# Cross attention on one core: every second exponential's bias on GpSimd, and the placing of the next queries split in two

## The reference

```python
q = (x @ Wq + bq).reshape(1, B * N, H, hd)
kv = (cond @ Wkv + bkv).reshape(1, -1, 2, H, hd)
q = _fq_sym(q * scale, axis=-1)          # rounded to 255 levels per row
k = _fq_sym(k, axis=-1)
v = _fq_sym(v, axis=2)
attn = jax.nn.softmax(jnp.einsum('bhqd,bhkd->bhqk', q, k), axis=-1)
attn = _fq_unsigned(attn, axis=-1)       # round(x / s) * s, s = row max / 255
out = jnp.einsum('bhqk,bhkd->bhqd', attn, v)
out = out.reshape(B, N, C) @ Wp + bp
```

## Time and profile before

| What | Value |
|---|---|
| Median of three runs | 994.36 us |
| The profiled execution's own time | 992.61 us |
| Its span in the trace | 990.7 us |
| Mean granted TensorE clock, share of full speed | 0.882 |
| VectorE busy, share of the span | 733.7 us, 74% |
| GpSimd busy | 564.7 us, 57% |
| ScalarE busy | 557.1 us, 56% |
| TensorE matmuls busy | 779.9 us, 79% |
| Stage of the 128 units (first score to last exponential) | about 653 to 849 us |
| VectorE, ScalarE, GpSimd busy from 740 to 760 us | 19.44, 16.98, 14.91 us of 20 |
| Granted clock from 740 to 760 us | 0.76 |

### The profile page before, as it was taken

The page is one execution under the profiler, slowest core; times in us unless marked ns, Lnnn a source line. Parts: engine busy times, 40 slices in busy tenths (PEclk is TensorE's granted clock), DMA queues, the critical chain, the costliest instruction groups (busy, mean ns, idle before and its releaser), DMA issues. The chain is left out here.

```text
span 990.7 us, 14021 instructions
## 1 busy us (share of the span) xinstructions
PE 779.9 (79%) x4673; PEld 500.3 (50%) x4673; DVE 733.7 (74%) x1291; ACT 557.1 (56%) x1028; POOL 564.7 (57%) x440
## 2 busy tenths in 40 slices
PE   4999999946877787778878978767777777789991
PEld 2554754425665666656763366623333333356551
DVE  4866258289999999999942555579999999454564
ACT  2324013278778777687741255479888888224540
POOL 3115200299999998999931033248777776315652
PEclk9999999969889989978989989967777777789996
DMA  5002030000000000000006000769999999422224
GB/s 175 1 6 81 1 133 2 0 1 1 1 0 1 1 1 1 1 0 1 1 1 229 0 1 1 266 120 176 186 182 167 172 174 173 83 86 75 78 74 159
DMA packets 149525, 69.61 MB, mean 70 GB/s; under 512 B 139003, under 2 KB 144909, under 8 KB 148302
## 3 DMA queue, kind: packets, MB, share of 16 engines
q1 hardware_dynamic: 147150, 62.42, 28.7%
q0 software_dynamic: 2304, 6.29, 2.1%
HBM read 27.46 MB, written 7.68 MB: 35 GB/s over the span
## 5 line engine op out<-in xcount | busy, mean ns | idle before, releaser
L749 POOL TENSOR_TENSOR r_pairs<-r_side_exp 128x945 f32<-128x945 f32 x128 | 225.2, 1794 | 0.0
L847 ACT ACTIVATE r_w<-r_w,r_scale 128x1001 f32<-128x1001 f32 (+1 forms) x128 | 144.9, 1135 | 71.8 <-DVE r_w L932 57.2
L1669 ACT ACTIVATE c_probs<-c_scores,c_bias,c_q_scale 128x1024 int16<-128x1024 f32 x128 | 154.2, 1205 | 30.0 <-DVE c_bias L1682 21.1
L804 PE MATMUL r_head_sum<-ident,r_w 128*128 128x128 f32 (+1 forms) x1024 | 136.7, 294 | 43.1 <-ACT ctxT L858 21.8
L1606 POOL CAST kv_parts<-c_probs 128x1024 bf16<-128x1024 int16 x128 | 132.4, 1041 | 54.7 <-ACT c_probs L1669 53.6
L1680 DVE TENSOR_REDUCE c_neg_max<-c_scores 128x1 f32<-128x1024 f32 x128 | 155.5, 1215 | 6.5 <-PE c_scores L1619 6.3
L804 PEld LDWEIGHTS r_head_sum<-ident,r_w 128*128 128x128 f32 (+1 forms) x1024 | 127.0, 155 | 61.0 <-issue 34.1
L1619 PE MATMUL c_scores<-c_kT,c_placed 128*128 128x512 bf16 x256 | 107.0, 513 | 49.5 <-ACT c_probs L1669 46.2
L924 DVE SCALAR_TENSOR_TENSOR r_chosen<-r_pairs,r_kept,r_z 128x1024 f32<-128x1024 f32 (+1 forms) x104 | 128.0, 1272 | 4.4 <-ACT r_pairs L837 2.5
L932 DVE TENSOR_TENSOR r_w<-r_pairs,r_chosen 128x1024 f32<-128x1024 f32 (+1 forms) x104 | 121.3, 1204 | 0.0
L780 PE MATMUL r_head_sum<-r_up,ctxT 128*128 128x256 f32 (+1 forms) x256 | 69.6, 439 | 22.5 <-ACT ctxT L858 22.5
(11 more groups left out here) (325 smaller groups left out, 1482.0 us busy)
## 6 DMA issues: line engine op xcount, KB each, us to landing
en_w<-in_w SPq DMA_DIRECT2D x1, 2992.0 KB, 12.1
ew_w<-in_w SPq DMA_DIRECT2D x1, 2992.0 KB, 12.3
ew_w_near<-in_w_near SPq DMA_DIRECT2D x1, 2176.0 KB, 21.3
r_up<-in_up SPq DMA_DIRECT2D x1, 2048.0 KB, 9.9
c_pT<-kv_parts SPq DMA_TRANSPOSE x128, 3.3
token_rows<-e_xn SPq DMA_DIRECT2D x2, 1024.0 KB, 5.8
e_row<-pick_rows SPq DMA_DIRECT2D x8, 256.0 KB, 4.2
zero_rows<-b_zeros SPq DMA_DIRECT2D x1, 1360.0 KB, 15.3
```

Of the source, the lines that this page charges most:

```text
L749: nc.gpsimd.tensor_tensor(pairs[:, v % MADE, BY_ACT * KEYS:].rearrange("p (a b) -> p a b", b=KEYS), a.broadcast_to([P, ROWS - BY_ACT, KEYS ...
L804: last = nc.tensor.matmul(head_sum[0:m, b // 4, (b % 4) * P:(b % 4 + 1) * P], w[:, v % RING, b * P:b * P + m], ident[:, :], start=(h == 0 ...
L847: nc.scalar.activation(w[:, v % RING, 0:COLS[f]], w[:, v % RING, 0:COLS[f]], ACT.Silu, scale=scale[:, t % 2, h:h + 1]).then_inc(silu_done, 1)
L1669: nc.scalar.activation(probs[:, u % RING, :], scores[:, u % SCORED, :, :].rearrange("p a b -> p (a b)"), ACT.Exp, bias=bias[:, t, h:h + 1] ...
```

## The change

Three things change.

1. In `attend` VectorE makes the bias of even units only. For odd units it makes the row maximum and signals `max_ready`; GpSimd makes the bias (`shift`), signals `pool_bias_ready`, and ScalarE waits for that. The bias of unit u+2 stands on GpSimd's stream behind the cast of unit u, for odd u; the one of unit 1 stands first.
2. The two copies of `place_queries` are parted: one before the cast of h = 4, one before that of h = 6. Each waits for the casts and the biases made so far.
3. Two semaphores go. VectorE's work on the decay waits for `phi_parts`, the first projection's relu, which stands behind the decay's exponential on ScalarE's stream. The keys' loads count on the same semaphore as the earlier weights, so that ScalarE and VectorE wait for the keys too.

```diff
-            dve.wait_ge(decay_exp, 1)
+            dve.wait_ge(phi_parts, 1)
...
-                sp.dma_start(keys[j * RETR:(j + 1) * RETR, :, j, :], i["keys"][j]).then_inc(keys_loaded, 16)
+                sp.dma_start(keys[j * RETR:(j + 1) * RETR, :, j, :], i["keys"][j]).then_inc(loaded, 16)
...
-            act.wait_ge(loaded, PRIVATE_LOADS)
+            act.wait_ge(loaded, PRIVATE_LOADS + 32)
...
-        PLACE_AT = 4
+        PLACE_AT = (4, 6)
...
+            def shift(u):
+                t, h = divmod(u, HEADS_C)
+                pool.wait_ge(max_ready, u // 2 + 1)
+                nc.gpsimd.tensor_scalar(bias[:, t, h:h + 1], neg_max[:, t, h:h + 1], s.q_scale[:, t, h:h + 1], LOG_LEVELS,
+                                        ALU.mult, ALU.add).then_inc(pool_bias_ready, 1)
+
+            shift(1)
             for u in range(UNITS_C):
                 t, h = divmod(u, HEADS_C)
-                if h == PLACE_AT and t + 1 < NT:
-                    pool.wait_ge(rounded_ready, u)
+                if h in PLACE_AT and t + 1 < NT:
                     if t >= 1:
                         pool.wait_ge(scored, HEADS_C * t)
-                    place_queries(nc, s, t + 1)
-                    pool.wait_ge(q_placed, 2 * (t + 2))
+                    own = PLACE_AT.index(h)
+                    pool.wait_ge(rounded_ready, u)
+                    pool.wait_ge(pool_bias_ready, (u + 2) // 2)
+                    place_queries(nc, s, t + 1, own)
+                    pool.wait_ge(q_placed, 2 * (t + 1) + own + 1)
                 pool.wait_ge(exp_done, u + 1)
...
                 nc.gpsimd.tensor_copy(rounded[:, u % ROUNDED, :], probs[:, u % RING, :]).then_inc(rounded_ready, 1)
+                if u % 2 == 1 and u + 2 < UNITS_C:
+                    shift(u + 2)
...
-                act.wait_ge(bias_ready, u + 1)
+                if u % 2 == 0:
+                    act.wait_ge(bias_ready, u // 2 + 1)
+                else:
+                    act.wait_ge(pool_bias_ready, u // 2 + 1)
...
-                chain.step(nc.vector.tensor_reduce(neg_max[:, t, h:h + 1], scores[:, u % SCORED, :, :].rearrange("p a b -> p (a b)"),
-                                                   AX.X, ALU.max, negate=True))
+                last = nc.vector.tensor_reduce(neg_max[:, t, h:h + 1], scores[:, u % SCORED, :, :].rearrange("p a b -> p (a b)"),
+                                               AX.X, ALU.max, negate=True)
+                if u % 2 == 1:
+                    last.then_inc(max_ready, 1)
+                    return
+                chain.step(last)
```

More of the change, by code:

```diff
@@ L196, in linear_attention @@
         loaded, consts = sem("loaded"), sem("consts")
-        decay_exp, projected = sem("decay_exp"), sem("projected")
+        projected = sem("projected")
         phi_parts, phi_done, kv_done = sem("phi_parts"), sem("phi_done"), sem("kv_done")
@@ L322, in _ @@
             act.wait_ge(loaded, 48)
-            nc.scalar.activation(decay[:, :], decay[:, :], ACT.Exp, scale=-1.0).then_inc(decay_exp, 1)
+            nc.scalar.activation(decay[:, :], decay[:, :], ACT.Exp, scale=-1.0)
             n = 0
@@ L577, in private_state @@
         loaded = pw.loaded
-        zeroed, keys_loaded = sem("zeroed"), sem("keys_loaded")
+        zeroed = sem("zeroed")
         sims_ready, up_ready, silu_ready, low_ready, done = (
@@ L600, in _ @@
             norm_tensor(nc, pe, ln, ident)
-            pe.wait_ge(loaded, PRIVATE_LOADS)
-            pe.wait_ge(keys_loaded, 32)
+            pe.wait_ge(loaded, PRIVATE_LOADS + 32)
             pe.wait_ge(ln.copied, ln.tiles + NT)
@@ L639, in _ @@
             nc.vector.tensor_copy(r.to_sims[:, :].rearrange("p (s n) -> p s n", s=2), low[:, :, 0:SIDE]).then_inc(copied, 1)
-            dve.wait_ge(loaded, PRIVATE_LOADS)
+            dve.wait_ge(loaded, PRIVATE_LOADS + 32)
             for h in range(NH):
@@ L1425, in _ @@
             pool.wait_ge(turned_copied, KV + 1)
-            place_queries(nc, s, 0)
+            for own in range(2):
+                place_queries(nc, s, 0, own)
             pool.wait_ge(s.placed_zeroed, 4)
@@ L1525, in _, with place_queries @@
                                       whole[:, :, 0:1, :].broadcast_to([P, QT * HEADS_C, PARTS - 2, HD_C])).then_inc(q_whole, 1)
[L1528 to L1532, removed]
+def place_queries(nc, s, t, own):
+    at = slice(own * P // 2, (own + 1) * P // 2)
+    nc.gpsimd.tensor_copy(s.placed[at, t % 2, :, own, :], s.qT[at, :, t * P:(t + 1) * P]).then_inc(s.q_placed, 1)
 def attend(nc, sh, s):
@@ L1563, in attend @@
         tail = ps("tail", [P, 1, HALF])
-        scored, bias_ready, exp_done, rounded_ready = sem("scored"), sem("bias_ready"), sem("exp_done"), sem("rounded_ready")
+        scored, max_ready, bias_ready, pool_bias_ready = sem("scored"), sem("max_ready"), sem("bias_ready"), sem("pool_bias_ready")
+        exp_done, rounded_ready = sem("exp_done"), sem("rounded_ready")
         turned = [sem("turned%d" % n) for n in range(IN_FLIGHT)]
```

## The result

The changed kernel is slower. Its median over 20 runs is 999.94 us, that of the kernel before, over as many, 995.33; the ratio is 1.0048 with a 95% interval from 1.0034 to 1.0062, so 3.4 to 6.2 us, about 4.8. I had forecast 1.2 us less.

A forecast was written before the change was run, and what follows sets the result against it. ScalarE and VectorE were both taken to pace units at 1.38 us, with 16.2 us lost; remaining losses of 7.6 + 29X gave a 1.2 us gain at X = 0.256: 991.4 us, 993.1 beside the median; 8-in-10 range 988.0 to 1000.0.

The forecast's parts named there:

- 6.24 + 29 x 0.267 + 1.33: Exponentials of the 128 units: forecast loss formula, tiles' delays plus a late score, with the measured GpSimd bias time put in.
- 2.44 + X against two steps, 2.76: GpSimd's path from one odd exponential to the next: an undisturbed pair is not slowed up to a bias time of 0.32.
- X: Time of one odd unit's bias on GpSimd, taken as 0.256 us from the nearest row; turning point 0.30.
- 0.20 + 2X: Delay in us at unit 7, behind the first placing copy, where `residual` has used up the lead at h = 4.
- 0.40 + X: Delay in us at unit 9, with the second placing copy standing between the biases of 7 and 9.
- `residual`: Extra VectorE job before h = 4: delay of 0.99 us before the change, forecast to leave 0.22.
- The lead of 0.64: Most by which a bias can come early at TensorE's high clock: 3.50 us against three steps of 4.14.
- the late `finish_b`: Late score at 778.95 that cost ScalarE 1.33 us; called TensorE's own and kept in the forecast.
- `scale_values`: Extra VectorE job before h = 15: delay of 0.52 us before, forecast to cost 0.10 + X a tile.
- The 0.6 of tile 1: Remaining loss of 0.6 us before the change, taken as one late-score delay in tile 1.
- ScalarE's 1.38: Spacing in us of undisturbed exponential starts, claimed as ScalarE's own floor, so that freeing VectorE only wins back lead.
- GpSimd becomes the bound: Rival: every odd exponential waits for GpSimd's longer bias; 998.0 or 1001.3 us; chance 0.30 for a longer bias.

The follow-up runs named there:

- e2: The kernel before with the two semaphore edits alone, against the kernel before: ratio 1.0000 (0.9976 to 1.0023).
- e5: The kernel before with no bias for odd units, whose exponential takes constants (output differs), against the kernel before: ratio 0.9973 (0.9953 to 0.9992).
- e8: The changed kernel with each bias on GpSimd made twice, first into a spare tile, against the kernel before: ratio 1.0251 (1.0218 to 1.0285).
- e3: The changed kernel without the placing copies of tiles 1 to 6 (output differs), against the kernel before: ratio 0.9953 (0.9931 to 0.9975).
- e9: The changed kernel with the biases of h = 5 and 7 made by VectorE again, against the kernel before: ratio 0.9997 (0.9973 to 1.0022).
- e1: The changed kernel again, no edit, against the kernel before: ratio 1.0054 (1.0033 to 1.0075), median 999.14 us.
- e6: Odd biases made by ScalarE itself, placing as in the kernel before, small edits in, against the kernel before: ratio 0.9970 (0.9945 to 0.9995).

## Why the prediction was wrong

Right were the price of the bias, 0.267 us for 0.256; the turn of the waits from VectorE to GpSimd; the places at which a copy hurts; and the late `a_k`, at 25.07. That the small edits cost nothing held in the whole time (e2); that the linear attention's end would not move did not. The direction and the sum were wrong. The step that failed is the new path through GpSimd: the sum put the handovers on that engine at nothing or too low, and with them the loop is longer than the old pace. Measured extra over 127 steps of 1.38 is 19.5 us; my sum gives 6.24 + 29 x 0.267 + 1.33 = 15.3. The 4.2 between them, term by term, each pair measured against 2.76:

- **The handovers on GpSimd.** I put the bias right behind the cast ("2.44 + X against two steps, 2.76. So up to X = 0.32 an undisturbed pair is not slowed"). A gap of 0.10 stands between cast and bias. With it the loop is 2.79, above 2.76, and every undisturbed pair costs 0.03 to 0.04: 1.4 us over 37 of them. In the earlier trace rows I had only casts in a row, which overlap by 0.05, and took that for all.
- **Placing.** "0.20 + 2X" and "0.40 + X" gave 0.73 and 0.67, and 0.61 and 0.67 in the first two tiles. Each is 0.85 to 0.88. Missing were 0.09 more ahead of the copy (0.16 idle) and 0.10 ahead of the bias. Over 14 copies: 12.2 instead of 9.6, 2.6 us.
- **`residual`.** I had 0.22 at h = 4; it is 0.45 to 0.59 in five tiles and 0.74 in tile 5, where a late score is in it: without that 3.2 us instead of 1.3, 1.9 more. The lead of 0.64 rested on three equal steps of 1.38. In the loop the steps are 1.60 and 1.20, so the three steps to an even unit are 4.00 and not 4.14, and its lead is 0.50. That gives 0.14 of the 0.3 that are missing in each; the rest is not traced.
- **On the other side**, the late `finish_b` that I kept with 1.33 leaves 0.3 in after, 1.0 less, and `scale_values` is 1.7 us instead of 2.6, as it shows in only five of seven tiles, 0.9 less. Why it does not in tiles 4 and 7 is not shown. The 0.6 of tile 1, which the sum counted as gained without a reason, did go.

The five come to 4.0; the rest to 4.2 is the first step (1.50) and rounding. So part of the miss was made good by luck: the handovers and the copies alone are 4.0, `residual` adds 1.9, and two terms that I had too high take as much off.

Under these terms lies one wrong reading, which did not set the sum but hid the choice. I took ScalarE's 1.38 for its own floor, because it equalled VectorE's and the trace showed no wait in it. It was VectorE's pace: in the earlier trace rows each exponential starts 0.25 after the bias does. In the trace of before the row sum's read-out ends 0.09 ahead of the next exponential, which starts at 762.62, a gap too short to be listed as a wait:

```profile
762.34 0.19 ACT L1669 ACTIVATION_READ_ACCUMULATOR c_probs<-c_scores,c_bias,c_q_scale 128x1 f32 x1
```

The next exponential can start while the read-out still runs (777.32 to 778.51 in after, and e5, steps of 1.20). The Trainium skill, ScalarE: Activation LUTs, section "What ACT_TABLE_LOAD costs", says that back-to-back activations overlap by about 93 ns; it does not speak of a read-out. If the read-out overlapped both its neighbours by as much, a step would be 1.20 + 0.19 less two overlaps, 1.2 us, an estimate; the trace of after has overlaps of 0.11 and 0.10 there and steps of 1.19 and 1.20. With such a floor, freeing VectorE looks like a large prize and not a small one, and the question becomes what the new path holds it back to.

The rival "GpSimd becomes the bound" was the right case with the wrong threshold: I let it decide from X = 0.30, and with the gaps it decides from X = 0.24 (2.76 - 1.35 - 1.04 - 0.10 - 0.03) for an undisturbed pair, and lower still where a copy stands in it. My estimate from the Trainium skill, GPSIMD Engine Reference, section "Performance pitfalls for Q7 kernels" (about 102 cycles for each small read command), put X above 0.3, but I counted three one-element operands where the instruction reads two from memory; two are 0.17 us by that figure, an estimate. So the 267 ns measured neither bear that rule out nor speak against it.

Shown by runs: the loop (e8), the copies' share (e3, e9), no cost of the small edits in the whole time within 2.3 us (e2), that ScalarE is not held to 1.38 (e5). The stage explains 3.3 us (3.2 to 3.7 with the stages of e1 and e2) of the 3.4 to 6.2 measured. Whether the 1.5 up to the middle value are real is open. Two things could be in them and no run parts them: the linear attention, which ends 0.2 to 1.5 us later where the edits are in, and the clock. Its mean over the executions is 0.880 in both sets of the changed kernel and 0.882 for the kernel before beside e1, whose 30 executions are about 0.5 us slower for each 0.001 less.

## What to carry to other kernels

Before work is moved to an engine that has idle time, write down the loop that it joins, with the gap of every handover, and compare the sum with the pace: 0.10 here and 0.16 there turned a small gain into a loss, though the engine was idle a quarter of the time. An engine whose every step starts a fixed time after another's may be following it, even where no wait is listed, and then its step is no floor. And an occasional job that was hidden behind an off-path engine stops being hidden when a critical instruction is queued behind it: those go elsewhere (e9), or the critical one does (e6).

## What the runs showed of the hardware

- GpSimd's multiply and add of 128x1 with two operands from memory took 266 to 268 ns, and two in a row without a wait follow at 0.34 us, 0.07 more than their length; two casts of 1.04 follow at 0.98 to 1.0, less than theirs.
- ScalarE's activation of 128x1 with two such operands took 378 ns, more than GpSimd's 267 and VectorE's 214.
- An exponential of 128x1024 with constants took 1012 ns, with bias and scale from memory 1203.
- The kernel before took 994 us on one chip and 1006 on two others. It was not profiled on those; in the versions that were, the stretch behind the routing's logits is 132 to 137 us, against 119 to 121 on the first.
